# A transformer layer on one core: in its expert stage VectorE moves the gathered rows, and the weighted rows get two buffers

## What is computed

```
x = x + cross_attention(layernorm(x), ctx)      # 16 heads of 64
x = x + causal_attention(layernorm(x))          # 16 heads of 64
x = x + moe(layernorm(x))
```

## Time and profile before

| What | Value |
|---|---|
| Median of 3 runs | 2422.04 us (2420.14 to 2428.12) |
| The profiled execution's own time | 2421.15 us |
| Its span, first to last instruction | 2419.4 us |
| Busy: PE, DVE, ACT, POOL | 93%, 63%, 52%, 37% of the span |
| Mean granted TensorE clock | 0.975 |
| Expert stage, first turn to last scatter's issue | 2013.8 to 2400.4 us |
| GpSimd busy in 50 us of that stage (2100 to 2150) | 39.2 us |
| TensorE busy in the same 50 us | 45.0 us |
| Output copied from acc, issue to landing | 9.6 us, behind the last scatter |

### The profile page before, as it was taken

How to read it: one execution, slowest core, us unless ns; L and a number is a source line. 1 busy time by engine, 2 the same in 40 slices (tenths; PEclk the granted TensorE clock), 3 DMA queues, 4 the chain that set the end, 5 groups by cost and what they waited for, 6 DMA issues and landing times. The chain is left out here.

```text
span 2419.4 us, 53231 instructions
## 1 busy us (share of the span) xinstructions
PE 2262.0 (93%) x18144; PEld 1982.8 (82%) x18144; DVE 1534.7 (63%) x3324; ACT 1266.7 (52%) x3832; POOL 902.5 (37%) x1141
## 2 busy tenths in 40 slices
PE   5999999999999999999996999999999866998895
PEld 4888888888888888888886999999999745777774
DVE  5656665666566666666556888889898673433331
ACT  4555555555555555555554667666666422433332
POOL 3333333333233333333332222222222225877784
PEclk9999999999999999999998999999999968999997
DMA  5000000000000000000001000000000103334324
GB/s 172 19 10 17 17 9 17 9 17 9 17 9 17 9 17 9 17 9 17 9 2 70 1 19 18 9 17 9 17 17 10 48 8 86 84 68 94 74 49 98
DMA packets 52933, 73.93 MB, mean 31 GB/s; under 512 B 9408, under 2 KB 36800, under 8 KB 52800
## 3 DMA queue, kind: packets, MB, share of 16 engines
q1 hardware_dynamic: 39952, 55.07, 7.1%
q0 software_dynamic: 12912, 17.98, 4.5%
HBM read 55.47 MB, written 21.76 MB: 32 GB/s over the span
## 5 line engine op out<-in xcount | busy, mean ns | idle before, releaser
L356 POOL TENSOR_TENSOR p_sb<-p_sb,rinv 128x512 f32<-128x512 f32 x256 | 284.1, 1110 | 837.3 <-DVE rinv L606 837.3
L528 ACT ACTIVATE p_sb<-s_ps,nmax 128x256 f32<-128x256 f32 x512 | 238.3, 470 | 426.7 <-DVE nmax L587 426.7
L749 POOL TENSOR_TENSOR sp_sb<-sp_sb,srinv 128x512 f32<-128x512 f32 x128 | 133.4, 1042 | 425.1 <-DVE srinv L935 425.1
L58 DVE SCALAR_TENSOR_TENSOR qbd_lo<-m_ps,qbd_hi 64x256 fp32r<-64x256 f32 x256 | 108.1, 422 | 227.4 <-ACT qbd_hi L46 225.7
L57 DVE TENSOR_TENSOR kt_lo<-k_ps,kt_hi 128x512 fp32r<-128x512 f32 x256 | 176.1, 688 | 110.8 <-ACT kt_hi L45 109.3
L45 ACT CAST kt_hi<-k_ps 128x512 fp32r<-128x512 f32 x256 | 151.5, 592 | 130.4 <-PE k_ps L65 129.9
L883 ACT ACTIVATE sp_sb<-sm_sb,snmax 128x128 f32<-128x128 f32 x512 | 199.4, 390 | 7.2 <-DVE snmax L946 4.1
L603 DVE COPY pt_sb<-t_ps 128x512 f32<-128x512 f32 x256 | 176.6, 690 | 38.3 <-PE t_ps L449 34.4
L587 DVE TENSOR_REDUCE nmax<-s_ps 128x2 f32<-128x512 f32 x256 | 174.0, 680 | 0.1
L57 DVE TENSOR_TENSOR e_ht_lo<-e_ht_ps,e_ht_hi 128x512 fp32r<-128x512 f32 x67 | 46.3, 691 | 184.6 <-ACT e_ht_hi L45 184.5
L449 PEld LDWEIGHTS t_ps<-ident,p_sb 128*128 128x128 f32 x1024 | 127.4, 140 | 35.0 <-issue 1.2
(11 more groups left out here) (280 smaller groups left out, 7542.4 us busy)
## 6 DMA issues: line engine op xcount, KB each, us to landing
ctx_raw<-in_ctx_t SPq DMA_DIRECT2D x32, 256.0 KB, 2.7
ctx_raw<-in_ctx_t SPq DMA_DIRECT2D x64, 128.0 KB, 2.8
xn<-f_xn SPq DMA_DIRECT2D x16, 256.0 KB, 2.2
acc<-x_sb SPq DMA_DIRECT2D x16, 256.0 KB, 2.3
e_raw<-in_gate SPq DMA_DIRECT2D x8, 512.0 KB, 4.0
e_raw<-in_up SPq DMA_DIRECT2D x8, 512.0 KB, 4.9
e_raw<-in_down SPq DMA_DIRECT2D x8, 512.0 KB, 6.4
x_sb<-in_x SPq DMA_DIRECT2D x1, 3584.0 KB, 15.4
```

Of the source, the lines that this page charges most:

```text
L356: nc.gpsimd.tensor_tensor(prob, prob, inv, ALU.mult).then_inc(norm_done, 1)
L528: ex = nc.scalar.activation(p_sb[:, k, b * J:(b + 1) * J], s_ps[1 - w][:, b * J:(b + 1) * J], ACT.Exp, bias=nmax[:, k, b:b + 1], scale=1.0 ...
L749: nc.gpsimd.tensor_tensor(prob, prob, inv, ALU.mult).then_inc(norm_done, 1)
```

## The change

VectorE takes over the move. It copies all 264 columns of a gathered row, so `e_xs` now has the weights too, and ScalarE copies them from there into `slot_weights`. The two gather buffers become one tensor with two halves, and the half is chosen by i % 2 in a register. The weighted rows `ys` get two halves as well, and `y_copy(i)` waits for the index copy of `add_rows(i-1)` (which itself comes after the landing of scatter i-2) in place of the landing of scatter i-1. The wait of `y_copy` for the weights is gone, as ScalarE writes them itself. On GpSimd the moves drop out; each gather(k) stands ahead of add_rows(k-5) and waits until VectorE has moved tile k-2. The counts for the tail change, and with an odd number of tiles one gather more is issued, for slots behind the last tile.

```
--- before.py
+++ after.py
@@ -1265,7 +1265,7 @@
                 link(V.tensor_tensor_scan(upto[:, 1:EXPERTS + 1], ones[:, 0:EXPERTS], tiles[:], 0.0, ALU.mult, ALU.add))
                 link(V.tensor_copy(first_tile[:], upto[:]))
                 link(V.tensor_scalar(pairs[:], first_tile[:, EXPERTS:EXPERTS + 1], 1, None, ALU.arith_shift_right))
-                link(V.tensor_scalar(first_left[:], pairs[:], 2.0, -3.0, ALU.mult, ALU.add))
+                link(V.tensor_scalar(first_left[:], pairs[:], 2.0, -5.0, ALU.mult, ALU.add))
                 link(V.tensor_scalar(last_tile[:], upto[:, 1:EXPERTS + 1], -1.0, None, ALU.add))
                 link(V.tensor_scalar(cnt[:], upto[:, 0:EXPERTS], float(P), None, ALU.mult))
 
@@ -1306,15 +1306,15 @@
             none = sbuf(ex, "e_none", [P, 1], mybir.dt.uint32)
             dummy = [sbuf(ex, f"e_dummy{i}", [P, 1]) for i in range(2)]
             token_out = sbuf(ex, "e_token_out", [P, 1], mybir.dt.uint32)
-            xs_in = [sbuf(ex, f"e_xs_in{i}", [P, ROW]) for i in range(2)]
-            xs_sb = sbuf(ex, "e_xs", [P, D])
+            xs_in = sbuf(ex, "e_xs_in", [P, 2 * ROW])
+            xs_sb = sbuf(ex, "e_xs", [P, ROW])
             xt_hi = sbuf(ex, "e_xt_hi", [P, D], F32R)
             xt_lo = sbuf(ex, "e_xt_lo", [P, D], F32R)
             silu_sb = sbuf(ex, "e_silu", [P, F])
             h_sb = sbuf(ex, "e_h", [P, F])
             ht_hi = sbuf(ex, "e_ht_hi", [P, F], F32R)
             ht_lo = sbuf(ex, "e_ht_lo", [P, F], F32R)
-            ys_sb = sbuf(ex, "e_ys", [P, D])
+            ys = sbuf(ex, "e_ys", [P, 2 * D])
             xt_ps = psum(ex, "e_xt_ps")
             g_ps = psum(ex, "e_g_ps")
             u_ps = psum(ex, "e_u_ps")
@@ -1370,27 +1370,19 @@
 
             @block.gpsimd
             def _(pool):
-                def gather(i, half):
-
-
-                    wait(pool, s_moved, i - 1 if isinstance(i, int) else i + -1)
+                def gather(i, half, freed):
+
+
+                    wait(pool, s_moved, freed)
                     nc.gpsimd.tensor_tensor(token_now[half][:], token_of[:, bass.ds(i, 1)], none[:], ALU.add).then_inc(s_now, 1)
                     pool.wait_ge(s_now, i + 1)
+                    wait(pool, s_dummy, i)
                     nc.gpsimd.tensor_tensor(dummy[half][:], zero[:], zero[:], ALU.add).then_inc(s_dummy, 1)
                     pool.indirect_dma_start(
-                        out=xs_in[half][:], out_offset=None, in_=xn_dram,
+                        out=xs_in[:, half * ROW:(half + 1) * ROW], out_offset=None, in_=xn_dram,
                         in_offset=bass.IndirectOffsetOnAxis(ap=token_now[half][:], axis=0)).then_inc(s_xs[half], DMA)
 
-                def move(i, pair, half):
-
-                    pool.wait_ge(s_xs[half], DMA * pair + DMA)
-                    wait(pool, s_dummy, i)
-                    nc.gpsimd.tensor_tensor(weight[:, bass.ds(i * EXPERTS, EXPERTS)], xs_in[half][:, D:ROW],
-                                            zero[:].to_broadcast([P, EXPERTS]), ALU.add).then_inc(s_weight, 1)
-                    wait(pool, xt_mm, i)
-                    nc.gpsimd.tensor_tensor(xs_sb[:], xs_in[half][:, 0:D], zero[:].to_broadcast([P, D]), ALU.add).then_inc(s_moved, 1)
-
-                def add_rows(i):
+                def add_rows(i, half):
 
                     wait(pool, s_added, DMA * i)
                     nc.gpsimd.tensor_tensor(token_out[:], token_of[:, bass.ds(i, 1)], none[:], ALU.add).then_inc(s_out_now, 1)
@@ -1399,31 +1391,29 @@
                     wait(pool, s_out_gate, i)
                     nc.gpsimd.tensor_tensor(out_gate[:], zero[:], zero[:], ALU.add).then_inc(s_out_gate, 1)
                     pool.indirect_dma_start(
-                        out=acc, out_offset=bass.IndirectOffsetOnAxis(ap=token_out[:], axis=0), in_=ys_sb[:],
+                        out=acc, out_offset=bass.IndirectOffsetOnAxis(ap=token_out[:], axis=0), in_=ys[:, half * D:(half + 1) * D],
                         in_offset=None, compute_op=ALU.add).then_inc(s_added, DMA)
 
                 more_pairs = pool.value_load(pairs[0:1, 0:1], min_val=MIN_TILES * EXPERTS // 2, max_val=MAX_TILES // 2)
                 nc.gpsimd.memset(none[:], 0).then_inc(s_zero, 1)
                 pool.wait_ge(s_zero, 2)
+                for i in range(6):
+                    gather(i, i % 2, i - 1)
+                add_rows(0, 0)
+                with pool.Fori(3, more_pairs) as j:
+                    for half in range(2):
+                        gather(2 * j + half, half, 2 * j + (half - 1))
+                        add_rows(2 * j + (half - 5), 1 - half)
+                left = pool.value_load(first_left[0:1, 0:1], min_val=MIN_TILES * EXPERTS - 6, max_val=MAX_TILES - 6)
                 for half in range(2):
-                    gather(half, half)
-                for half in range(2):
-                    move(half, 0, half)
-                    gather(2 + half, half)
-                for half in range(2):
-                    move(2 + half, 1, half)
-                    gather(4 + half, half)
-                add_rows(0)
-                with pool.Fori(2, more_pairs) as j:
-                    for half in range(2):
-                        move(2 * j + half, j, half)
-                        gather(2 * j + (2 + half), half)
-                        add_rows(2 * j + (half - 3))
-                for half in range(2):
-                    move(2 * more_pairs + half, more_pairs, half)
-                not_added = pool.value_load(first_left[0:1, 0:1], min_val=MIN_TILES * EXPERTS - 4, max_val=MAX_TILES)
-                with pool.Fori(not_added, tile_count(pool)) as i:
-                    add_rows(i)
+                    gather(left + (5 + half), half, left + (4 + half))
+                    add_rows(left + half, 1 - half)
+                with pool.Fori(left + 7, tile_count(pool) + 2) as i:
+                    gather(i, 0, left + 6)
+                for k in range(2, 5):
+                    add_rows(left + k, 1 - k % 2)
+                with pool.Fori(left + 5, tile_count(pool)) as i:
+                    add_rows(i, 0)
 
             @block.tensor
             def _(pe):
@@ -1486,6 +1476,7 @@
                     act.wait_ge(xt_mm, i + 1)
                     wait(act, u_mm, i)
                     split_hi_act(nc, xt_hi[:], xt_ps[:, 0:D]).then_inc(xt_h, 1)
+                    nc.scalar.copy(weight[:, bass.ds(i * EXPERTS, EXPERTS)], xs_sb[:, D:ROW]).then_inc(s_weight, 1)
 
                 def rest(i):
 
@@ -1500,9 +1491,8 @@
 
                 def y_copy(i, e):
                     act.wait_ge(y_mm, i + 1)
-                    act.wait_ge(s_weight, i + 1)
-                    wait(act, s_added, DMA * i)
-                    nc.scalar.activation(ys_sb[:], y_ps[:, 0:D], ACT.Copy,
+                    wait(act, s_out_now, i)
+                    nc.scalar.activation(ys[:, bass.ds((i % 2) * D, D)], y_ps[:, 0:D], ACT.Copy,
                                          scale=weight[:, bass.ds(i * EXPERTS + e, 1)]).then_inc(y_copied, 1)
 
                 def tile(i, before, e, e_before, piece):
@@ -1527,6 +1517,15 @@
 
             @block.vector
             def _(dve):
+                def move(i):
+
+                    half = i % 2
+                    dve.wait_ge(s_xs[0], DMA * (i // 2) + DMA)
+                    wait(dve, s_xs[1], DMA * ((i + 1) // 2))
+                    wait(dve, s_weight, i)
+                    wait(dve, xt_mm, i)
+                    nc.vector.tensor_copy(xs_sb[:], xs_in[:, bass.ds(half * ROW, ROW)]).then_inc(s_moved, 1)
+
                 def xt_lo_copy(i):
                     dve.wait_ge(xt_h, i + 1)
                     split_lo_dve(nc, xt_lo[:], xt_ps[:, 0:D], xt_hi[:]).then_inc(xt_l, 1)
@@ -1545,14 +1544,18 @@
                     ht_lo_copy(before)
                     product(i)
                     xt_lo_copy(i + 1)
+                    move(i + 2)
                     if piece is not None:
                         dve.wait_ge(s_whi, PIECES * (e + 1) + piece + 1)
                         cut = slice(piece * CUT, (piece + 1) * CUT)
                         split_lo_dve(nc, w_lo[:, (e + 1) % 2, cut], raw[:, cut], w_hi[:, (e + 1) % 2, cut]).then_inc(s_wlo, 1)
 
+                move(0)
                 xt_lo_copy(0)
+                move(1)
                 product(0)
                 xt_lo_copy(1)
+                move(2)
                 last = run_tiles(dve, tile)
                 ht_lo_copy(last)
```

## The result

The changed kernel takes 2393.7 us (median of 4 runs, 2391.8 to 2395.39) against 2421.56 for the kernel before, measured anew beside it: 27.9 us less, a ratio of 0.9876 (95% interval 0.9859 to 0.9894). The forecast was 2389, range 2374 to 2411.

The account below looks back on a forecast made before the run. Before, GpSimd was taken as full in ordinary tiles, with late landings and weight pieces on top; afterwards VectorE's move decides. 66 x 5.17 = 341.2 against 370.3 gives -29.1, ends -2.9, from 2421.15 to 2389 us; range 2374 to 2411.

Parts of the forecast that it names:

- The new period: TensorE turn to turn: 3.72 to the product, 1.10 to VectorE's move, 0.30 copy, 0.05 to the turn; 5.17 us.
- the short rows: VectorE copies of 8 and 64 columns, 173 and 194 ns; they put the 264-column move at about 0.28 us.
- the 407 ns row: VectorE operation on 256 columns with one tensor read, taken as the move's upper bound, 0.42 us.
- rival 2: VectorE's sequencer, between split's wait and move, is the bound: 2428 us, chance 0.05; middle case 2411, as much again.
- The second buffer: Two buffers of weighted rows let ScalarE's copy ride over six late scatter landings: the 15 us go.
- GpSimd's catching up: Scatter chain of 4.6 us against 5.1: a 2.5 us backlog melts by 0.5 a tile, over five or six tiles.
- an ordinary tile wins nothing: In an ordinary tile VectorE's move comes as late as GpSimd's did, at a period of 5.17 us.
- piece tiles: 21 tiles where VectorE splits a piece of the next expert's weights, lengthening a GpSimd copy by up to 1.0 us.
- Ends: First two moves of the expert stage -0.9 us, its last tiles and scatters about -2; together -2.9.
- Rival 1: GpSimd and VectorE exclude each other, so a DMA issue holds off the move: 13 + 8 us, 2410; chance 0.2.
- rival 4: The second buffer hides nothing, as scatters stay one behind another and their chain bounds: 2398 us, chance 0.05.
- rival 3: TensorE becomes the bound, 4.98 to 4.89 us a tile: 2374 us, chance 0.12.

Follow-up runs that it names:

- e3: The changed kernel with VectorE's copy of the rows made twice, first into a tile nobody reads: 2409.35 us, ratio 0.9951.
- e6: The changed kernel with VectorE's move ahead of the product and ScalarE's copy of the eight weights ahead of silu: 2401.1 us, ratio 0.9916.
- e4: The kernel before with the weights of experts 1 to 7 not loaded, three 4 KB transfers in their place: 2409.65 us, ratio 0.9948.
- e5: The changed kernel with the weights of experts 1 to 7 not loaded, three 4 KB transfers in their place: 2388.74 us, ratio 0.9862.
- e1: The kernel before with two buffers of weighted rows and nothing else, the move staying on GpSimd: 2409.51 us, ratio 0.9947.
- e2: The changed kernel with one buffer of weighted rows, the move on VectorE: 2419.0 us, ratio 0.9986.
- e7: The changed kernel with move ahead of product, weights copy ahead of silu, and scatter's index copy ahead of the wait for the landing before: 2372.0 us, ratio 0.9792.

## Why the prediction was right

**The new period.** The forecast 3.72 + 1.10 + 0.30 + 0.05 = 5.17 came out as 3.72 + 0.98 + 0.30 + 0.13 = 5.13 in the tile above, as 3.72 + 1.03 + 0.30 + 0.13 = 5.18 in the median and 5.20 on average. The tile e_xs after, min, median and max of the durations:

```profile
L1527 DVE COPY e_xs<-e_xs_in x69: 286/298/583, 2015.9 to 2366.2; 128x264 f32 x63, 128x264 f32<-128x264 f32 x6
L1479 ACT COPY slot_weights<-e_xs x68: 198/199/201, 2017.3 to 2365.5; 128x8 f32 x63, 128x8 f32<-128x8 f32 x5
```

The copy takes 298 ns for 264 columns, as the short rows said and not as the 407 ns row did. Against the 194 ns for 64 columns that is 0.52 ns for each further column; the 407 ns row gives 1.11, about twice as much. The Trainium skill, page VectorE: DVE Perf Modes, section Mode 2×_2P, gives two columns per cycle for such a copy; the 298 ns agree with it. The move starts 1.03 us after the product in the median, 0.94 to 1.43, between my 0.93 and 1.57: the register work of its sequencer is mostly hidden, and rival 2 fell with that. Two terms were mis-sized: the move's start, 1.03 where I had 1.10, and the last one, 0.13 where I had 0.05. They cancel, so that 5.17 was met to a hundredth is luck; the mechanism is not. e3 shows that the chain is the bound, e6 that the tile falls to 4.88 once the move leaves it.

**The second buffer.** Right in what it hides: the loads cost 10.7 us before and 1.6 after by e4 and e5, or 14.3 and nothing by the six late tiles alone. I had 15, from six landings at their full 2.5 us. Of GpSimd's catching up I had the wrong pace: behind a late landing scatters are issued 4.75 to 5.0 us apart, 4.87 on average, not 4.6, so it recovers 0.3 us a tile, not 0.5. It was enough for the 1.8 us of a late one, but takes six of the eight tiles between two loads.

**What bounded the kernel before.** Here my reading was half right. I said GpSimd's own work of 5.15 us was the bound of the ordinary tile and the landing only of the stretched ones. e1 and e2 put GpSimd at 5.0 and the scatter's chain at 5.3. The tile that I took for ordinary stands right behind a late landing, as the first row here shows; two turns far from any load, the other rows, are 5.27 us apart.

```profile
2182.74 0.47 ACT L1505 ACTIVATE e_ys<-e_y_ps,slot_weights 128x256 f32<-128x256 f32 x1 [4.73 <-DMA acc<-e_ys,e_token_out]
...
2131.01 0.43 PE L1434 MATMUL e_xt_ps<-ident,e_xs 128*128 128x128 f32 x2 [0.30 <-POOL e_xs L1391]
...
2136.28 0.43 PE L1434 MATMUL e_xt_ps<-ident,e_xs 128*128 128x128 f32 x2 [0.22 <-POOL e_xs L1391]
```

So the step "an ordinary tile wins nothing" failed: by the table above ordinary tiles went from 5.33 to 5.22 us, some 4 us of the gain, and the 21 piece tiles held 8 us where I had put most of the remaining 15. That it changed nothing in the sum is luck: I took 66 new tiles from the measured 370.3 us, whatever that was made of. It would have misled me on either part alone, and did: both my numbers for e1 and e2 missed.

**Ends.** -1.0 and -2.3 against -0.9 and -2. The profiled execution lies 4.6 us above the forecast (2393.78 us): 2.9 of it come from the code ahead of the stage, 2.1 from the turns (343.3 us against 341.2).

**Rival 1, GpSimd against VectorE.** Answered by rows of the changed kernel: a scatter's issue and a move inside it, such a pair where the move is long, and a piece of weights beside an index copy.

```profile
2287.60 1.60 POOL L1393 DMA_INDIRECT acc<-e_ys,e_token_out  x1 [0.43 <-issue]
...
2288.69 0.30 DVE L1527 COPY e_xs<-e_xs_in 128x264 f32 x1
...
2064.70 1.60 POOL L1393 DMA_INDIRECT acc<-e_ys,e_token_out  x1 [0.44 <-issue]
...
2065.32 0.58 DVE L1527 COPY e_xs<-e_xs_in 128x264 f32 x1
...
2289.16 1.31 POOL L1377 TENSOR_TENSOR e_token_now<-token_of,e_none 128x1 uint32<-128x1 uint32 x1
...
2289.21 1.23 DVE L57 TENSOR_TENSOR e_w_lo<-e_raw,e_w_hi 128x1024 fp32r<-128x1024 f32 x1 [0.23 <-ACT e_w_hi L45]
```

In 51 of 69 moves a scatter's issue was under way, far more than I had thought, since the scatters run later than I placed them. The first pair shows a move of 0.30 us wholly inside one. Only eight of the 51 are longer. The six that began 0.61 to 0.83 us into the issue all ended 1.20 us into it, and one that began at 0.90 took its 0.30 us: as if the port were taken for a short stretch up to about 0.9 us. The other two began at 1.29 and 1.33 and ended at 1.68. Together the eight cost 1.4 us, not 21. The last pair is the other direction: beside e_w_lo the index copy takes 1.31 us in place of 0.19. The Trainium skill, page SBUF — State Buffer, section SBUF: two separate sides, describes a lock held for the whole instruction. The last pair agrees with that; the issue of a DMA is not excluded as a whole by these rows. Nor did the moves hold up the scatters: their issue takes 1.60 us in the mean, as before the change, and the median landing 3.83 us, before and after.

**Rivals 3 and 4** did not come in the changed kernel. Both are real one step further: e6 is bound by the scatters as in rival 4, e7 by TensorE as in rival 3.

## What to carry to other kernels

Where two chains through the same loop have nearly the same length, undo each part of a double change alone before you price it: here 12 and 3 us became 28, and of two further steps one alone lost 7 and the other alone won at most 2.5, while the pair won 22. A queue of transfers that must follow one another needs time to spare in each round, or each late landing reaches the end in full; here that spare time was worth more than a tile 0.3 us shorter. And an instruction that only needs early inputs belongs ahead of the one that its engine waits for: the move stood behind the product only by the order in the file.

## What was unexpected of the hardware

A VectorE copy of 264 f32 columns between SBUF tensors runs undisturbed (0.30 us) inside most of GpSimd's 1.60 us issue of an indirect DMA. It was longer only when it began 0.61 to 0.83 us into the issue, and then ended 1.20 us into it, or when it began at 1.29 to 1.33 us, and then ended at 1.68. And six loads of 1.5 MB cost one late landing each (5.6 to 6.0 us) in the changed kernel, but in e6, where scatters follow each other at 4.9 us without a gap, six of 6.6 to 6.9 us and three more over 4.5. What decides how late a scatter lands and whether a second one is caught was not tried. Last, in e6 the lower clock came with five standstills of TensorE of 2.3 to 2.6 us, so that a tile behind a late one could be longer too (5.90 us against 4.87).
